# Softmax attention: where in a slot TensorE multiplies the values

## The reference

```python
q = (x @ Wq.T).reshape(B, S, H, hd).transpose(0, 2, 1, 3)      # k, v likewise
att_rel_pos = jnp.einsum('bhsd,pd->bhsp', q, pos_emb_k)
att_idxs = jnp.clip(ar[None, :] - ar[:, None], -r, r - 1) % P   # r = 128, P = 256
att_pos = att_rel_pos[:, :, ar[:, None], att_idxs]
attn_val = jnp.einsum('bhqd,bhkd->bhqk', q, k)
att = jax.nn.softmax((attn_val + att_pos) * attn_scale, axis=-1)
y = jnp.einsum('bhqk,bhkd->bhqd', att, v)
```

## Time and profile before

| | |
|---|---|
| median of three runs | 1197.96 us |
| the profiled execution | 1194.37 us |
| its span | 1192.6 us |
| softmax stage, first to last exp | 457.6 to 916.9 us of the span |
| TensorE matmul busy over the span | 1026.4 us (86%) |
| ScalarE | 729.6 us (61%) |
| VectorE | 755.5 us (63%) |

### The profile page before, as it was taken

How to read it: one execution, slowest core, us unless ns; L and a number is a source line. 1 busy time by engine, 2 the same in 40 slices (tenths; PEclk the granted TensorE clock), 3 DMA queues, 4 the chain that set the end, 5 groups by cost and what they waited for, 6 DMA issues and landing times. The chain is left out here.

```text
span 1192.6 us, 22324 instructions
## 1 busy us (share of the span) xinstructions
PE 1026.4 (86%) x7844; PEld 648.4 (54%) x7844; DVE 755.5 (63%) x1671; ACT 729.6 (61%) x1096; POOL 540.1 (45%) x723
## 2 busy tenths in 40 slices
PE   1499999999996548999999999999998178999997
PEld 1344444777774524554555555455544156878785
DVE  6145241677876247787788888777771056676766
ACT  1289988555553126777777777777765065555453
POOL 1166776465553130444434333333223187655554
PEclk9999999999998557999999999999999599999999
DMA  5521231644563297888888888888740554433443
GB/s 132 227 85 53 64 119 45 150 121 137 164 187 107 98 257 246 246 239 242 243 238 242 241 243 238 244 244 243 224 139 11 169 168 120 124 116 121 116 122 94
DMA packets 147132, 197.42 MB, mean 166 GB/s; under 512 B 34361, under 2 KB 113562, under 8 KB 146970
## 3 DMA queue, kind: packets, MB, share of 16 engines
q1 hardware_dynamic: 125868, 184.98, 50.8%
q0 software_dynamic: 21152, 11.01, 5.6%
HBM read 123.00 MB, written 72.74 MB: 164 GB/s over the span
## 5 line engine op out<-in xcount | busy, mean ns | idle before, releaser
L977 ACT ACTIVATE a_probs<-a_duo 128x1024 f32<-128x1024 f32 x256 | 261.7, 1025 | 80.5 <-PE a_duo L910 79.6
L1376 POOL TENSOR_TENSOR f_hid_lo<-f_hid,f_hid_hi 128x512 fp32r<-128x512 f32 (+1 forms) x168 | 216.6, 1291 | 147.6 <-ACT f_hid_hi L1347 147.6
L826 POOL DMA_DIRECT2D scr_y1c<-ys x256 | 126.7, 504 | 252.4 <-DVE ys L1005 240.1
L1029 DVE TENSOR_REDUCE a_part<-a_duo 128x2 f32<-128x1024 f32 (+3 forms) x256 | 215.5, 855 | 12.2 <-PE a_duo L885 10.8
L1022 DVE CUSTOM_DVE_ANT_0 a_band_sum<-a_duo,a_rel_raw 128x256 f32<-128x256 f32 (+2 forms) x320 | 131.4, 448 | 87.8 <-PE a_duo L885 58.2
L973 ACT ACTIVATE a_rel<-a_rel_ps 128x384 f32<-128x384 f32 x246 | 120.3, 489 | 55.4 <-PE a_rel_ps L872 39.3
L636 ACT ACTIVATE a_probs<-a_duo 128x1024 f32<-128x1024 f32 x192 | 139.7, 830 | 21.5 <-PE a_duo L585 20.1
L925 PE MATMUL a_acc_ps<-a_probs,a_v 128*32 128x256 f32 x2048 | 143.7, 387 | 0.1
L872 PE MATMUL a_rel_ps<-emb_all,a_q 31*128 31x384 f32 x247 | 112.8, 457 | 28.9 <-ACT a_rel L973 11.6
L574 POOL TENSOR_TENSOR a_probs<-a_probs,const 128x256 f32<-128x256 f32 x128 | 100.1, 798 | 58.4 <-ACT a_probs L636 58.1
L1495 DVE TENSOR_TENSOR f_u<-f_u,f_gate 128x512 f32<-128x512 f32 (+1 forms) x100 | 69.7, 697 | 86.6 <-PE f_u L1250 45.5
(11 more groups left out here) (235 smaller groups left out, 1932.5 us busy)
## 6 DMA issues: line engine op xcount, KB each, us to landing
scr_rel<-a_rel SPq DMA_DIRECT2D x128, 384.0 KB, 3.8
a_rel_raw<-scr_rel SPq DMA_DIRECT2D x128, 384.0 KB, 4.5
w_share<-scr_cw SPq DMA_DIRECT2D x128, 128.0 KB, 3.2
f_share<-scr_cw SPq DMA_DIRECT2D x40, 256.0 KB, 3.2
scr_y1c<-ys POOLq DMA_DIRECT2D x256, 8.0 KB, 3.7
f_raw<-in_w SPq DMA_DIRECT2D x21, 192.0 KB, 3.3
f_share<-scr_cw SPq DMA_DIRECT2D x20, 192.0 KB, 2.9
f_share<-scr_cw SPq DMA_DIRECT2D x16, 224.0 KB, 3.0
```

The costliest lines, as they stand in the source:

```text
L826: pool.dma_start(scr["y1c"][w, b, head, :, at:at + QUARTER], ys[32 * (2 * hd + c) + HD * w:32 * (2 * hd + c) + HD * (w + 1), h % 2, :]).th ...
L977: act.activation(probs[:, n % KEPT, :], bank_pair("t", n)[:], ACT.Exp, scale=SCALE).then_inc(exp_done, 1)
L1029: ins = dve.tensor_reduce(part[:, h % 2, x, :, j % 4], both[:, :, lo * P:hi * P], AX.X, ALU.max, negate=True)
L1376: pool.tensor_tensor(hid_lo[0:m, n % 4, :], hid[0:m, n % 2, :], f32(hid_hi[0:m, n % 4, :]), ALU.subtract).then_inc(lo_ready, 1)
```

## The change

In each slot the loop over `values` moves from the end of TensorE's slot, behind the turned scores, the band's transposes and the small transpose, to the place between `scores` and `turned`. No instruction is added or taken away. VectorE, ScalarE, GpSimd and SyncE have the same program.

```diff
                 if 0 <= m < SLOTS:
                     scores(m)
+                if n >= 0:
+                    while valued < min(n - 1 if n >= SLOTS else n // 16 * 16 + sum(VALUES[:n % 16 + 1]) - 3, SLOTS):
+                        values(valued)
+                        valued += 1
                 if 0 <= n < SLOTS:
                     if n % 8 == 0:
                         pe.wait_ge(row_stored[n // 8 % 2], 32 * (n // 16 + 1))
@@
                     pe.transpose(max_rows, negmax[:, h % 2, :, :].rearrange("p a b -> p (a b)"), ident).then_inc(row_ready, 1)
-                if n >= 0:
-                    while valued < min(n - 1 if n >= SLOTS else n // 16 * 16 + sum(VALUES[:n % 16 + 1]) - 3, SLOTS):
-                        values(valued)
-                        valued += 1
             weights_turned(router, sb, pe, banks)
```

## The result

The changed kernel took 1217.56 us, the median of runs from 1210.12 to 1218.33, against 1199.11 us before. The ratio is 1.0146, with an interval from 1.0105 to 1.0187, so it is slower by 18 us. The prediction was 1209 us, slower, within 1189 to 1222. The profiled execution of the changed kernel took 1210.12 us with a span of 1208.3, 15.7 us more than the span before.

What follows compares the result with a forecast made beforehand. TensorE was taken as the bound, at full clock. 14.4 cycles x 0.78 = +11.3 us on 1194.4 gave 1205.7 for the profiled execution, which lay 3.6 under the median: 1209 us, range 1189 to 1222.

Steps and rivals of the forecast that it cites:

- The walk: Start-to-start prices summed through one 16-slot cycle on TensorE in the new order: +0.65 us, a cycle of 29.90.
- The loop of 2.0 us over ScalarE: Turned scores (n), exp, copy of next offsets, then offsets (n+2): 2.0 us plus the band, with values now standing in it.
- the wait for `ys`: Slot 10: values opening a new sum wait for VectorE's copy of the old one; 0.5 us of that pair's +0.60.
- one more switch: A switch is TensorE going from one tile shape to another, priced 0.14 us; slots with values and band go from three to four.
- The correction: Old-order walk gave 28.98, not 29.25, so like with like +0.92; the middle with +0.65, 0.78 a cycle, was taken.
- a granted clock under 1.00: Named as a sign in the softmax stage that would upset the whole forecast; no size given.
- the late copy: Slot 11: as before but for a late ScalarE copy, 2.38 against 2.29 us, +0.09.
- The switches alone: Five more changes of tile shape a cycle, 5 x 0.14 = 0.7 us; by this rule alone 10 us slower.
- The filled waits: Rival: gains in slots 0, 3, 7 stay, derived ScalarE and `ys` losses don't bind; -15 us, 1183 us, chance 0.15.
- the third rival: Turned scores don't overlap the next slot's blocks: 0.7 us a cycle, 10 us on top, 1219 us; chance 0.12.
- The second rival: It cancels: half the derived waits occur, cycle 29.05 to 29.35, between -3 and +1.5 us, 1197 us; chance 0.24.

Runs made afterwards that it cites:

- halved exp: Exp of only half the columns, in the changed kernel and, as control, in the kernel before; one run each, 1200.05 and 1190.13 us.
- slot 10 put back: The changed kernel with slot 10's values behind the band again; 1205.61 us, ratio 1.0083 to the kernel before.
- the two split kernels: Values ahead only from slot 32 on, and only in the first 32 slots; ratios to the kernel before 1.0076 and 1.0083.

## Why the prediction was right, and where not

*The walk.* Every step of it can be laid beside the changed profile. The column measured has differences of medians over thirteen cycles of either kernel:

| slots | predicted | measured |
|---|---|---|
| 0, 1 | -0.47 | -0.44 |
| 2, 3 | -0.07 | -0.06 |
| 4 | 0 | -0.01 |
| 5, 6 | +0.23 | +0.23 |
| 7 | -0.46 | -0.45 |
| 8 | +0.26 | +0.26 |
| 9, 10 | +0.60 | +0.57 |
| 11 | +0.09 | -0.02 |
| 12, 13 | +0.30 | +0.33 |
| 14, 15 | +0.18 | +0.21 |

The walk gave a cycle of 29.90 and the trace has 29.85. The loop of 2.0 us over ScalarE (halved exp) and the wait for `ys` (slot 10 put back) each have a run that isolates them. The loss in slot 8 is read from the changed profile alone; it comes from one more switch and from lost overlap, since three blocks that took 0.60 together now take 0.43 and 0.43 in two parts. The medians add up to +0.62 and not to 0.68, since the last four cycles before were shorter, 28.95 to 29.08.

*The correction was wrong.* "Like with like the cost is +0.92" and the middle of 0.78 rested on the old order's walk falling 0.27 short. The shortfall belonged to the old order and didn't carry over: measured is 0.68. The term 14.4 x 0.78 = 11.3 should have been 14.4 x 0.68 = 9.8, or some 9 in this trace, whose last part of a cycle (slots 224 to 229) has mostly the slots that gain. Slot 11 did not grow. Halved exp shortens it by 0.09 with values ahead and not with values behind, so the late copy is there, and something that was not traced gives as much back.

*The start was mis-sized.* The step that failed is in the sum: it let all 14.4 cycles run at the full clock, since the windows that it read lay at 600 to 640 us. The text named a granted clock under 1.00 as what would upset it, but it put no price on it. The first cycle cost +9.1 us, of which the walk's own share is 0.7 at the full clock. The timed rounds of the two split kernels put the early slots at 8 to 10 us and the steady ones at about 9. The two errors had opposite signs and the second was larger: the profiled execution took 1210.1 us where 1205.7 was forecast. The other half of the miss is the step from there to the median of the runs, 7.4 us where 3.6 was added. The forecast so fell 8.6 us short. The mechanism that it describes accounts for about half of the slow-down; that the range took in the other half too is in part luck.

*The switches alone.* By them the cost would have been 10 us, near the steady part. That nearness is chance. Slot 10 put back takes away one switch and 0.55 us, and halving exp takes away no switch and 1.40 us. A price of the switch itself can be seen only where nothing else waits, in slot 8, and there it is not apart from the lost overlap.

*The rivals.* The filled waits won in slots 0, 1 and 7 and hardly in others (slots 2 and 3 gained 0.06), and a kernel with only slots 0 and 7 moved shows that this rival was right about the place and wrong about the change as a whole. Turned scores do overlap the next slot: they start at 630.44, scores at 630.57 and offsets at 630.78, so the third rival falls. Here the trace has the scores start 0.21 ahead of the offsets, though the program writes the offsets first; it does so, by 0.2 to 0.3, in slots 6, 10, 13 and 15 of all thirteen cycles of the changed kernel, and nowhere in the kernel before. The order of recorded starts is thus not always that of the program, and the starts of these four slots are late by as much, which the pairs of the table even out. The second rival falls too, since every slot but 11 came out within 0.03 us of the walk.

*What stays open* is the clock at the start. With the old order in the first 32 slots it rose near 461, 466, 469, 472, 479 and 482 us in six profiles; with values ahead in any of them near 481, 482, 483, 490, 502 and 503. Four of them:

| kernel | order in the first cycle | clock rises near | slots 0 to 16 |
|---|---|---|---|
| before | old | 461.5 us | 29.93 us |
| before, again | old | 469 us | 31.41 us |
| slots 0 and 7, from slot 32 | old | 482 us | 36.87 us |
| changed | new | 481.5 us | 39.05 us |

So the order seems to shift the rise, and something else scatters it by as much: the 20 us between the first profiles of the two kernels are no measure of what the order does. The timed rounds of the kernel with only the first 32 slots ahead show that the early order costs some 10 us. Two cycles of it at the clocks of the changed profile make 2.2 + 0.7 us; that the rest is a later rise in the timed rounds too is inferred from the profiles. Why values ahead of the turned scores should hold the clock down longer was not found.

## What to carry to other kernels

When filler work is moved ahead of an instruction that waits, ask first who waits for that instruction: here exp, the copy behind it on ScalarE and the offsets two slots later closed a loop of 2.0 us in which the filler then stood. Move it only in the slots where the wait is long and the slots behind have slack in the loop. The filler may even be longer than the wait: in slots 0 and 7 TensorE waited some 0.45 us (turned scores 0.88 and 0.89 behind the offsets, of which 0.43 is work), the values take 1.00 and 0.57, and both gained. Slots 5 and 14, with waits that come out under 0.2 us in the same way, lost through the loop. Two of ten slots gave 1%, all ten cost 1.5%. Walk one whole period with start-to-start prices for the new order, and look at the granted clock of the first periods as well as of the middle.

## What the hardware showed that was not expected

- A block of matmuls of one tile shape costs 0.12 to 0.14 us beside its work, at the full clock, when the next block has another shape. Within one shape, blocks in other row groups start 0.01 to 0.34 us apart: offsets, scores and turned scores of slot 8 took 0.60 us together and 0.86 with values between them.
- TensorE can be recorded busy for 19.63 of 20 us (460 to 480 us in the changed kernel) and still be granted 0.50; with slots 0 and 7 ahead from slot 32 on, so in the old order at that point, it was 19.50 of 20 us.
- In mid-stage, with TensorE busy 4.63 and then 4.92 of 5 us, the clock fell to 0.50 for some 14 us, and a cycle grew from 28.2 to 33.7 us. Dips in mid-stage stood in four of twelve profiles: two long ones with slots 0, 3 and 7 ahead, and one of 3 to 4 us each in the kernel before again, ahead before slot 32, and slots 0 and 7 ahead (670 to 675 us, mean 0.66), where a cycle grew by 1.3 to 1.5 us. Their cause was not looked for, and the timed rounds don't show how often they come there.
